# Self-attention stages: which engine copies the turned probabilities out of PSUM

## The chip, the cores and the metric

The kernel runs on one NeuronCore of a Trainium2 chip. The metric is the device time of one execution in microseconds (us). The core has five instruction queues that matter here: TensorE (PE, matrix products and transpositions), VectorE (DVE), ScalarE (ACT), GpSimd (POOL) and SyncE (SP, which issues DMA transfers). Each queue is worked in order, and the queues meet at semaphores.

## The reference

The program is a decoder of four layers over `x` of shape (8, 100, 256): eight sequences of 100 tokens. Each layer has a self-attention (or a substitute for it), a cross-attention and a feed-forward part, twelve stages in all. Three of the stages contain a softmax self-attention with 16 heads of 16 features: `L0_attn`, the inner attention of `L1_ffn` (with relative positions), and a convolved one in `L2_xattn`. What they compute, per sequence and head, is

```python
att = softmax((q @ k.T + positions_or_mask) * scale, axis=-1)   # 100 x 100
out = concat_heads(att @ v) @ wo                                # 100 x 256
x   = layernorm(x + out)
```

The change touches the first two. They are called the first stage (tile names `l0a_`, 19.5 to 108 us of the trace) and the second stage (`l1f_`, 946.8 to 1052 us).

## The kernel before, in words

All three attentions are built by `self_heads` (line 1310). It treats one sequence of the batch per **turn** j, and the 16 heads of a sequence as four **groups** of four heads (G = 4), numbered g = 4j + r. `grouped` (line 1332) is true for the first two stages: there the four heads of a group are exponentiated by one instruction, and GpSimd subtracts the row extremum before it. A group passes through these steps:

1. `scores(j)`, line 1545, TensorE: 32 small products into four PSUM banks, for all four groups of a sequence at once. It waits until the maxima of all groups of the sequence before are done, since these read the banks.
2. `maxima(g)`, line 1777, VectorE: adds mask or positions, writes `s_sb` and the row extremum `nmax`; four pairs of instructions per group. In the second stage the positions come by DMA (`l1f_bd`, line 1421).
3. `shift(g)`, line 1454, GpSimd: subtracts the extremum.
4. `exponentials(g)`, line 1678, ScalarE: one exponential over 100x400 into `probs`. There are three slots of `s_sb` and `probs`.
5. `sums(g)`, line 1793, VectorE: row sums; `inverses(j)`, line 1797, after the fourth.
6. `turn(g)`, line 1569, TensorE: transposes the four heads into PSUM bank 4 or 5, by the parity of g. It waits until the group two before has been copied out of that bank.
7. `copy_turned(g)`: copies the 100x400 result from PSUM to `probsT`. **Even groups are copied by VectorE (line 1786), odd ones by ScalarE (line 1694).** Each counts up a semaphore of its own, `even_copied` or `odd_copied`.
8. `values(j)`, line 1581, TensorE: waits for both counts, and multiplies all four groups with the values.

After that follow, one or two turns behind: `inv` (line 1499, copied by ScalarE on line 1655), `outputs` (line 1802, VectorE), `y` (line 1504, TensorE: output projection), `add_output` (line 1808 with the statistics of lines 114 and 116, VectorE), the reciprocal root on GpSimd (lines 136 and 138), `normalise_vector` (line 123, VectorE), and `turn_x` (line 1509, TensorE, stored by ScalarE on line 1664, in the second stage by two instructions on line 1660). `y`, `inv`, `turn_x`, the values of the next sequence (`v`, line 1489) and a late part of the keys (`k`, line 1484) share one PSUM bank in a fixed order (`wait_side`).

The order on each engine is written out by hand, one `for j in range(B + 2)` loop per engine. In a turn of the grouped stages:

- VectorE: maxima(4j), sums(4j-2), sums(4j-1), inverses(j-1), **copy_turned(4j-2)**, maxima(4j+1), add_output(j-2), maxima(4j+2), normalise(j-2), sums(4j), maxima(4j+3), **copy_turned(4j)**, copy_values(j+1), sums(4j+1), outputs(j-1).
- ScalarE: exponentials(4j), copy_turned(4j-1), exponentials(4j+1), inv(j-1), exponentials(4j+2), a copy of keys in turns 0 and 1, exponentials(4j+3), copy_turned(4j+1), turn_x(j-2).
- TensorE: turn(4j-2), y(j-2), turn(4j-1), values(j-1), inv(j-1), turn(4j), v(j+1), keys in turns 0 and 1, scores(j+1), turn(4j+1), turn_x(j-2).
- GpSimd: shift(4j), widen(j-1) (line 1461), shift(4j+1), the root for j-2, shift(4j+2), shift(4j+3).

Of the kernel before, what the change touches and what calls it, by code (L numbers as in the profile page):

```python
# [14 lines left out]
ACT = mybir.ActivationFunctionType  # L15
AX = mybir.AxisListType

B, S, D = 8, 100, 256
# [1291 lines left out]
def self_heads(nc, st, name, w, bias=None, mask=None, conv=None, xT=None, inner=None, between=None):  # L1310

    H, HD = 16, 16
    G = PER_QUAD
# [5 lines left out]
    with ExitStack() as ctx:  # L1319
        def sb(n, shape, dt=F32):  # L1320
            return ctx.enter_context(nc.sbuf_tensor(f"{name}_{n}", shape, dt))
# [7 lines left out]
        probsT = sb("probsT", [S, 2, G, G * S])  # L1329
        nmax = sb("nmax", [S, 3, G])  # L1330
        rsum, rinv = sb("rsum", [S, B, H]), sb("rinv", [S, B, H])
        grouped = conv is None
# [18 lines left out]
        with stage_sems(nc, sems + stored_sems + NORM_SEMS) as s, nc.Block(no_gpsimd_drain=True) as block:  # L1351
# [3 lines left out]
            turned_tile = lambda g: st.ps[0:S, T_BANK + g % 2, 0:G * S]  # L1355
# [285 lines left out]
            def _(act):  # L1641
# [47 lines left out]
                def copy_turned(g):  # L1689
                    j, r = divmod(g, G)  # L1690
                    act.wait_ge(s.turned, g + 1)
                    if j >= 2:
                        act.wait_ge(s.values_done, j - 1)
                    act.activation(probsT[:, j % 2, r, :], turned_tile(g), ACT.Copy).then_inc(s.odd_copied, 1)

                for part in range(KT):
                    copy_out("k", 0, part)
# [6 lines left out]
                for j in range(B + 2):  # L1704
                    if conv and 1 <= j <= B:
                        exponentials(G * j - 1)
                    if not conv and j < B:
                        exponentials(G * j)
                    if 1 <= j <= B:
                        copy_turned(G * j - 1)  # L1710
                    if j < B:
                        if conv:
                            exponentials(G * j)
                        else:
                            exponentials(G * j + 1)
                    if 1 <= j <= B:
                        copy_out("inv", j - 1)
                    if j == 0 and not between:
                        copy_q(1)
                    if j < B:  # L1720
                        exponentials(G * j + (1 if conv else 2))
                    if j < KT:
                        copy_out("k", 1, j)
                    if j < B:
                        exponentials(G * j + (2 if conv else 3))
                    if j < B:
                        copy_turned(G * j + 1)
                    if j >= 2:
                        copy_out("turn_x", j - 2)

            @block.vector
            def _(dve):
# [48 lines left out]
                def copy_turned(g):  # L1781
                    j, r = divmod(g, G)
                    dve.wait_ge(s.turned, g + 1)
                    if j >= 2:
                        dve.wait_ge(s.values_done, j - 1)
                    dve.tensor_copy(probsT[:, j % 2, r, :], turned_tile(g)).then_inc(s.even_copied, 1)
# [8 lines left out]
                def inverses(j):  # L1795
                    dve.wait_ge(s.summed if grouped else s.exp_done, G * (j + 1))
                    dve.reciprocal(rinv[:, j, :], rsum[:, j, :]).then_inc(s.inv_ready, 1)
# [21 lines left out]
                for j in range(B + 2):  # L1819
                    if j < B:  # L1820
                        if conv:
                            keep(G * j)
                            keep(G * j + 1)
                        else:
                            maxima(G * j)
                    if j == 0 and not between:
                        copy_q(1)
                    if 1 <= j <= B:
                        sums(G * j - 2)
                        sums(G * j - 1)  # L1830
                        inverses(j - 1)
                        copy_turned(G * j - 2)
                    if j < B:
                        maxima(G * j + (0 if conv else 1))
                        if conv:
                            keep(G * j + 2)
                    if j >= 2:
                        add_output(j - 2)
                    if j < B:
                        maxima(G * j + (1 if conv else 2))  # L1840
                    if j < B:
                        if conv:
                            keep(G * j + 3)
                    if j >= 2:
                        if inner:
                            dve.wait_ge(s.x_summed, j - 1)
                        normalise_vector(dve, norm, s, j - 2)
                    sums(G * j)
                    if j < B:
                        maxima(G * j + (2 if conv else 3))  # L1850
                    if conv and 1 <= j <= B:
                        outputs(j - 1)
                    if j < B:
                        copy_turned(G * j)
                    if j + 1 < B:
                        copy_values(j + 1)
                    if conv and j < B:
                        maxima(G * j + 3)
                    sums(G * j + 1)
                    if not conv and 1 <= j <= B:  # L1860
                        outputs(j - 1)
# [2638 lines left out]
```

## Time and profile before

| | |
|---|---|
| median of 3 runs | 2467.63 us (2466.69 to 2467.66) |
| profiled execution | 2466.49 us |
| its span, first to last instruction | 2464.7 us |
| PE busy | 2074.1 us (84%) |
| DVE busy | 1566.5 us (64%) |
| ACT busy | 1062.5 us (43%) |
| POOL busy | 730.9 us (30%) |
| mean granted TensorE clock | 0.902 |

The profiled execution lies 1.14 us below the median, and its span 1.8 us below its own time. The shares of busy time are means over twelve stages with different limits; the two stages of the change take some 190 of the 2465 us. In the views below, a bracket behind a row tells how long the engine stood idle before the instruction and who released it. "PEclk" and granted clock are the TensorE clock as a share of its higher level of 2.4 GHz: 1.00 is that level, 0.50 the lower one of 1.2 GHz.

### The profile page before, as it was taken

To read this page: it belongs to the slowest core of one execution; us is meant where nothing else is said; L and a number is where in the kernel's file an instruction comes from. 1 tells how busy PE (TensorE), PEld (TensorE's weight loads), DVE (VectorE), ACT (ScalarE), POOL (GpSimd) and SP (SyncE) were. 2 spreads that over 40 slices of the span, in tenths; PEclk is the share of its full clock that TensorE was granted. 3 is DMA by queue.
4 is the path that set the end of the run, shared out by engine and by line. 5 is a ranking of instruction groups with operands and counts; after the bars stand their busy time and mean duration, and the time that the engine had idled before them with its cause. 6 is when DMAs were issued, how large, how long until landed. Compare 5 with 4: busy or idle time off the path is not lost. (4 is left out here: it accounts for less than half of the span.)

```text
span 2464.7 us, 41893 instructions
## 1 busy us (share of the span) xinstructions
PE 2074.1 (84%) x14482; PEld 1633.6 (66%) x14482; DVE 1566.5 (64%) x3664; ACT 1062.5 (43%) x2704; POOL 730.9 (30%) x933
## 2 busy tenths in 40 slices
PE   6799578898999984779778969989996899798994
PEld 4567444555666653579756638879995567598893
DVE  5767767895666653755555544556554567557995
ACT  3266456662344442323211635524432367455662
POOL 3543119993000011400122420000002565213546
PEclk9899789999999986889877979979997899798997
DMA  2077126671111125234200024333210367355772
GB/s 117 17 113 109 50 112 171 186 203 66 43 43 46 43 74 167 43 142 153 90 11 5 1 57 115 88 101 97 88 56 29 55 109 102 97 166 180 248 233 82
DMA packets 142725, 240.90 MB, mean 98 GB/s; under 512 B 46999, under 2 KB 108539, under 8 KB 140488
## 3 DMA queue, kind: packets, MB, share of 16 engines
q1 hardware_dynamic: 140492, 235.24, 34.6%
q0 software_dynamic: 2048, 3.29, 0.4%
q8 instruction: 104, 1.70, 0.3%
q14 instruction: 81, 0.66, 0.1%
HBM read 198.35 MB, written 40.12 MB: 97 GB/s over the span
## 5 line engine op out<-in xcount | busy, mean ns | idle before, releaser
L2064 ACT ACTIVATE l1x_probs<-ps,l1x_nmax 100x361 f32<-100x361 f32 x128 | 70.8, 559 | 166.0 <-DVE l1x_nmax L2137 166.0
L2573 POOL TENSOR_TENSOR l1a_dbx<-l1a_dx,l1a_rows 128x400 f32<-128x400 f32 x128 | 130.8, 1049 | 3.0 <-DVE ps L2631 2.2
L2661 PE MATMUL ps<-l1a_zc,tables_sb 128*128 128x400 f32 x256 | 111.1, 519 | 20.4 <-DVE l1a_hs L2618 9.3
L2649 PE MATMUL ps<-ctxT,weights 128*128 128x361 f32 x256 | 101.8, 489 | 10.3 <-PEq L2341 9.3
L3278 PE MATMUL ps<-l3f_routed_x_high,l3f_routed_w_low 128*128 128x128 f32 x320 | 91.5, 286 | 15.4 <-DVE l3f_routed_w_low L3342 14.0
L2855 PE MATMUL ps<-l2f_x_high,l2f_w_high 128*128 128x400 f32 x272 | 95.2, 350 | 0.0
L1145 ACT ACTIVATE l3x_probs<-l3x_s_sb,l3x_nmax 100x361 f32<-100x361 f32 x128 | 75.3, 590 | 44.8 <-DVE l3x_nmax L1250 44.8
L2854 PE MATMUL ps<-l2f_x_high,l2f_w_low 128*128 128x400 f32 x272 | 94.7, 348 | 0.0
L2856 PE MATMUL ps<-l2f_x_low,l2f_w_high 128*128 128x400 f32 x272 | 94.6, 348 | 0.0
L2631 DVE TENSOR_TENSOR_SCAN ps<-ps,l1a_dbx 128x400 f32<-128x400 f32 x86 | 81.8, 986 | 14.5 <-ACT ps L2596 7.3
L3280 PE MATMUL ps<-l3f_routed_x_low,l3f_routed_w_high 128*128 128x128 f32 x320 | 90.8, 284 | 0.0
L3279 PE MATMUL ps<-l3f_routed_x_high,l3f_routed_w_high 128*128 128x128 f32 x320 | 90.8, 284 | 0.0
L1143 ACT ACTIVATE l0x_probs<-ps,l0x_nmax 100x361 f32<-100x361 f32 x128 | 71.0, 562 | 36.8 <-DVE l0x_nmax L1257 36.7
L2661 PEld LDWEIGHTS ps<-l1a_zc,tables_sb 128*128 128x128 f32 x256 | 47.9, 195 | 58.6 <-DVE l1a_zc L2613 17.2
L136 POOL TENSOR_SCALAR l1x_heads_all_vareps<-l1x_heads_all_meanvar 100x1 f32<-100x1 f32 x8 | 1.7, 218 | 279.8 <-DVE l1x_heads_all_meanvar L116 279.8
L2594 ACT ACTIVATE ps<-l1a_delta,weights 128x400 f32<-128x400 f32 x128 | 76.2, 595 | 19.6 <-DVE ps L2631 11.7
L2649 PEld LDWEIGHTS ps<-ctxT,weights 128*128 128x128 f32 x256 | 50.8, 199 | 50.6 <-issue 15.0
L3011 DVE SCALAR_TENSOR_TENSOR l2f_hg<-ps,l2f_biases,l2f_act_out 128x800 f32<-128x800 f32 x34 | 35.7, 1051 | 73.1 <-PE ps L2856 73.1
L3374 POOL TENSOR_TENSOR l3f_routed_w_low<-ctxT,l3f_routed_w_high 128x1024 fp32r<-128x1024 f32 x20 | 49.5, 2475 | 110.2 <-ACT l3f_routed_w_high L3317 110.2
L2137 DVE TENSOR_REDUCE l1x_nmax<-ps 100x2 f32<-100x722 f32 x64 | 58.0, 906 | 34.5 <-PE ps L2000 34.3
L1557 PE MATMUL ps<-l2x_a_kept,l2x_a_taps 100*100 100x100 f32 x768 | 76.0, 258 | 3.0 <-DMA l2x_a_taps<-l2x_taps_spread 2.6
L1557 PEld LDWEIGHTS ps<-l2x_a_kept,l2x_a_taps 100*100 100x100 f32 x768 | 74.3, 174 | 5.5 <-DMA l2x_a_taps<-l2x_taps_spread 3.3
(735 smaller groups left out, 6650.2 us busy)
## 6 DMA issues: line engine op xcount, KB each, us to landing
l1a_rows<-l1a_rows_spilled SPq DMA_DIRECT2D x64, 400.0 KB, 4.4
ctxT<-l_ffn_units SPq DMA_DIRECT2D x20, 1026.0 KB, 5.8
l3f_expert<-l_ffn_units SPq DMA_DIRECT2D x20, 1026.0 KB, 5.9
l2x_a_taps<-l2x_taps_spread SPq DMA_DIRECT2D x8, 1912.5 KB
l2f_landing<-l_ffn_units SPq DMA_DIRECT2D x17, 771.0 KB, 5.4
l1f_gates<-l1f_gates SPq DMA_DIRECT2D x16, 800.0 KB, 4.1
l1x_keys<-l1a_key_sb SPq DMA_DIRECT2D x64, 180.5 KB, 4.6
l1x_kT<-l1x_keys SPq DMA_DIRECT2D x64, 180.5 KB, 2.3
```

The lines of the kernel that those rows point to most:

```text
L1557: last = pe.matmul(score_bank(r)[:, n, :], taps[:, j % 2, first:first + S], kept[:, g % 3, n, c:c + S], start=(c == 0), stop=(c == 2))
L2573: pool.tensor_tensor(dbx[:, n % BUFS, :], dx[:, m, :], rows[:, g % RING, 0, :], ALU.mult).then_inc(s.dbx_ready, 1)
L2594: act.activation(da(n), delta_h[:, m, j, :], ACT.Exp, scale=a_log[:, m, i:i + 1]).then_inc(s.da_ready, 1)
L2631: dve.tensor_tensor_scan(z(n), da(n), dbx[:, n % BUFS, :], 0.0, ALU.mult, ALU.add).then_inc(s.scan_done, 1)
L2649: last = pe.matmul(key_bank(u), w_key[:, k, pair * P:(pair + 1) * P], st.ctxT[:, b, k, :], start=(k == 0), stop=(k == KT - 1))
L2661: pe.matmul(y_bank(m), st.ident, zc[:, n % DONE, :], start=(i == 0), stop=(i == NS - 1)).then_inc(s.sum_done, 1)
L2854: pe.matmul(out, r(w_lo), r(x_hi), start=start, stop=False)
L2855: pe.matmul(out, r(w_hi), r(x_hi), start=False, stop=False)
L2856: return pe.matmul(out, r(w_hi), r(x_lo), start=False, stop=stop)
L3278: pe.matmul(out, r(lo), r(x_high[i % 2][:, k, :]), start=(k == 0), stop=False)
L3279: pe.matmul(out, r(hi), r(x_high[i % 2][:, k, :]), start=False, stop=False)
L3280: last = pe.matmul(out, r(hi), r(x_low[i % 2][:, k, :]), start=False, stop=(k == KT - 1))
```

## The change

In the grouped stages ScalarE makes all 32 copies of turned probabilities of a stage, where it made the 16 of the odd groups; the 16 of the even groups leave VectorE. ScalarE's `copy_turned` now counts up the semaphore of the group's parity. copy_turned(4j-2) stands at the head of ScalarE's turn, before exponentials(4j); copy_turned(4j) stands between exponentials(4j+2) and exponentials(4j+3), behind the copy of the keys in turns 0 and 1. The convolved stage keeps its order.

```diff
@@ block.scalar
-                    act.activation(probsT[:, j % 2, r, :], turned_tile(g), ACT.Copy).then_inc(s.odd_copied, 1)
+                    act.activation(probsT[:, j % 2, r, :], turned_tile(g), ACT.Copy).then_inc((s.even_copied, s.odd_copied)[g % 2], 1)
...
                     if conv and 1 <= j <= B:
                         exponentials(G * j - 1)
+                    if grouped and 1 <= j <= B:
+                        copy_turned(G * j - 2)
                     if not conv and j < B:
                         exponentials(G * j)
...
                     if j < KT:
                         copy_out("k", 1, j)
+                    if grouped and j < B:
+                        copy_turned(G * j)
                     if j < B:
                         exponentials(G * j + (2 if conv else 3))
@@ block.vector
                         inverses(j - 1)
-                        copy_turned(G * j - 2)
+                        if not grouped:
+                            copy_turned(G * j - 2)
...
-                    if j < B:
+                    if not grouped and j < B:
                         copy_turned(G * j)
```

## Rows read from the trace of the kernel before

**Rows 1.** Window, its length, busy PE, PEld, DVE, ACT, POOL, then PEclk: first stage

```profile
40.71:84.88 44.17, 31.86 (x474) 24.14 (x474) 42.39 (x225) 17.72 (x40) 22.89 (x35) 1.00 0.01 2
```

**Rows 2.** Grouped lines of the first stage: busy us, mean ns, idle before

```profile
L1777 DVE CUSTOM_DVE_ANT_0 l0a_s_sb<-ps,tables_sb 100x100 f32<-100x100 f32 x128 | 25.4, 255 | 6.6 <-PE ps L1545 6.6
L1786 DVE COPY l0a_probsT<-ps 100x400 f32<-100x400 f32 x16 | 8.6, 540 | 1.2 <-PE ps L1569 1.2
L1694 ACT ACTIVATE l0a_probsT<-ps 100x400 f32<-100x400 f32 x16 | 8.0, 501 | 4.2 <-PE ps L1569 3.7
```

**Rows 3.** Timeline of DVE, first stage, one turn: start us, us

```profile
49.57 0.25 DVE L1777 CUSTOM_DVE_ANT_0 l0a_s_sb<-ps,tables_sb 100x100 f32<-100x100 f32 x1
...
51.54 0.51 DVE L1786 COPY l0a_probsT<-ps 100x400 f32<-100x400 f32 x1
51.97 0.25 DVE L1777 CUSTOM_DVE_ANT_0 l0a_s_sb<-ps,tables_sb 100x100 f32<-100x100 f32 x1
...
56.12 0.25 DVE L1777 CUSTOM_DVE_ANT_0 l0a_s_sb<-ps,tables_sb 100x100 f32<-100x100 f32 x1
...
56.84 0.56 DVE L1786 COPY l0a_probsT<-ps 100x400 f32<-100x400 f32 x1
57.33 0.41 DVE L1751 COPY l0a_vals<-ps 100x256 f32<-100x256 f32 x1
...
58.40 0.25 DVE L1777 CUSTOM_DVE_ANT_0 l0a_s_sb<-ps,tables_sb 100x100 f32<-100x100 f32 x1
```

**Rows 4.** Timeline of PE, first stage: values, scores and output around that turn's end

```profile
54.55 1.11 PE L1489 MATMUL ps<-weights,XT 128*100 128x256 f32 x4 [0.19 <-ACT l0a_r_sb L1655]
57.07 0.96 PE L1545 MATMUL ps<-l0a_kT,l0a_q_pad 32*100 32x100 f32 x32 [1.41 <-DVE l0a_nmax L1777]
...
59.33 1.11 PE L1504 MATMUL ps<-weights,l0a_o_norm 128*100 128x256 f32 x4 [0.31 <-ACT XT L1664]
```

**Rows 5.** Timelines of PE and DVE, first stage: maxima that waited for scores

```profile
39.68 0.96 PE L1545 MATMUL ps<-l0a_kT,l0a_q_pad 32*100 32x100 f32 x32
...
40.71 0.26 DVE L1777 CUSTOM_DVE_ANT_0 l0a_s_sb<-ps,tables_sb 100x100 f32<-100x100 f32 x1 [1.88 <-PE ps L1545]
```

**Rows 6.** Timelines of ACT and POOL, first stage, the end of that turn

```profile
58.95 0.33 ACT L1664 ACTIVATE XT<-ps 128x200 f32<-128x200 f32 x1
...
59.29 0.85 POOL L1454 TENSOR_TENSOR l0a_s_sb<-l0a_s_sb,l0a_nmax 100x400 f32<-100x400 f32 x1 [1.43 <-DVE l0a_nmax L1777]
...
60.17 0.54 ACT L1678 ACTIVATE l0a_probs<-l0a_s_sb 100x400 f32<-100x400 f32 x1 [0.90 <-POOL l0a_s_sb L1454]
```

**Rows 7.** Timelines of ACT and PE, first stage, turn 1

```profile
33.75 0.48 ACT L1694 ACTIVATE l0a_probsT<-ps 100x400 f32<-100x400 f32 x1
...
34.33 0.89 PE L1581 MATMUL ps<-l0a_probsT,l0a_vals 100*32 100x100 f32 x32 [1.20 <-DVE l0a_probsT L1786]
```

**Rows 8.** Timeline of PE, end of the first stage

```profile
94.40 2.03 PE L1504 MATMUL ps<-weights,l0a_o_norm 128*100 128x256 f32 x4 [0.67 <-ACT XT L1664]
```

**Rows 9.** Busy time by window, second stage: turns 3 to 6 together, turn 5

```profile
988.34:1027.10 38.76, 28.49 (x379) 21.44 (x377) 34.26 (x182) 16.42 (x37) 21.03 (x32) 0.91 0.32 67
1007.78:1017.29 9.51, 6.37 (x96) 4.79 (x94) 8.47 (x46) 4.15 (x10) 5.26 (x8) 0.99 0.32 68
```

**Rows 10.** Timeline of DVE, second stage

```profile
978.82 0.26 DVE L1777 CUSTOM_DVE_ANT_0 l1f_s_sb<-ps,l1f_bd 100x100 f32<-100x100 f32 x1 [15.05 <-DMA l1f_bd<-l1f_positions]
...
986.05 0.25 DVE L1777 CUSTOM_DVE_ANT_0 l1f_s_sb<-ps,l1f_bd 100x100 f32<-100x100 f32 x1
...
1020.69 0.42 DVE L1808 TENSOR_TENSOR l1f_heads_all_resid<-ps,X 100x256 f32<-100x256 f32 x1 [0.20 <-PE ps L1504]
```

**Rows 11.** Timeline of PE, second stage: values, scores, output

```profile
984.75 1.86 PE L1489 MATMUL ps<-weights,l1f_xT 128*100 128x256 f32 x4
...
996.50 1.65 PE L1545 MATMUL ps<-l1f_kT,l1f_q_pad 32*100 32x100 f32 x32 [1.77 <-DVE l1f_nmax L1777]
...
1018.66 1.99 PE L1504 MATMUL ps<-weights,l1f_o_norm 128*100 128x256 f32 x4 [0.25 <-ACT l1f_xT L1660]
```

## The prediction

> **What bounds the kernel now.** I read the stages one by one, because the change touches two of twelve. First the busy time by window, with one window per turn, then grouped lines, then the timelines of single engines over one turn, since the question is which wait ends last there.
>
> In the first stage, turns 2 to 6 take 44.17 us together, 8.83 us each, and VectorE is busy for 42.39 of them; ScalarE only for 17.72 [rows 1]. In the timeline VectorE's instructions follow one another with hardly a gap, so **VectorE sets the turn**. The copies to be moved are 16 of 0.54 us on VectorE; the like copy on ScalarE takes 0.50 [rows 2]. TensorE waits for VectorE: before the scores of the next sequence it stands idle for 1.41 us, until the last maxima of this one are done [rows 4].
>
> The second stage is different at its start: the first maxima of turn 2 wait 15.05 us for the positions' transfer and begin at 978.82 us [rows 10]. What is saved ahead of that is lost. From turn 3 on it is the first stage again: four turns take 38.76 us, a clean one 9.51, with VectorE busy for 8.47 of it [rows 9].
>
> **The change, part by part.** *What leaves VectorE.* In its queue an instruction costs the distance between starts, not its duration. copy_turned(4j-2) starts at 51.54 and the maxima behind it at 51.97: 0.43 us. copy_turned(4j) starts at 56.84 and its successor at 57.33: 0.49 us [rows 3]. If nothing else ended later, a turn would take 8.83 - 0.92 = 7.91 us.
>
> *What is late next.* The scores of the next sequence can only start when the maxima of 4j+3 are done, and the next maxima need the scores. From rows: those maxima begin at 56.12 [rows 3], the scores at 57.07 and take 0.96 [rows 4], so 0.95 + 0.96. Where maxima did wait, they began 0.07 us after the scores' end (39.68 + 0.96 = 40.64, then 40.71) [rows 5]. That makes 1.98 us from one group of maxima to the next sequence's first. VectorE now takes 58.40 - 56.12 = 2.28 us for this piece [rows 3]; without the copy it takes 1.79. So 0.19 us of the second copy comes back as a wait for scores: a turn of **8.10 us, 0.73 less**. Bounds of this term: 0 if the scores start sooner, 0.19 as taken.
>
> *Is TensorE ready to start the scores earlier?* The product before them, the next values, starts at 54.55 and ends at 55.66 [rows 4]; the scores would start 0.43 us sooner, at 56.64. Relative to the previous scores that chain doesn't move, and the turn may shorten by 1.41 us before it touches. The output projection ends at 59.33 + 1.11 = 60.44, 4.32 us after the maxima's 56.12 [rows 3, 4]; the new VectorE order wants it 1.98 us and then 2.68 us after those maxima (51.97 - 49.57 = 2.40, less the copy's 0.43, and 0.72 for one more group of maxima as between 56.12 and 56.84 [rows 3]), that is at 4.66. No wait.
>
> *What ScalarE gains.* Two copies of 0.50 us per turn [rows 2] on an engine that is busy for 3.5 of 8.8 us [rows 1]. What matters is who stands behind them. copy_turned(4j-2) stands before exponentials(4j): ScalarE is free for it when the XT store ends, 58.95 + 0.33, and done with it some 0.4 us later, at about 59.7. The input of the exponentials, the shift on GpSimd, ended at 60.14 and the exponentials began at 60.17 [rows 6]; in the new order the shift ends 0.30 us sooner, at 59.84. The copy fits with about 0.1 us to spare. In the second stage the store is two activations (line 1660); with 0.33 us for the second, as here, the exponentials would start up to 0.3 us late; who waits for them is the row sum five VectorE steps later and a transposition more than 2 us later, so I take 0 and keep 0.3 us a turn as the upper bound. copy_turned(4j) stands before exponentials(4j+3), whose input comes 1.74 us after the group's maxima began (58.40, 60.14 [rows 3, 6]); its transposition is over before those maxima start, so it is done in time. values(j) is released by the odd copy on ScalarE at 33.75 + 0.48 = 34.23, followed by the product at 34.33 [rows 7], although the profile names VectorE's copy there: the even copies are not what ends last, and none of their 0.54 us can be won at that place. No DMA and nothing on SP or GpSimd is moved; the convolved stage keeps its code.
>
> *Sum of the first stage.* Turn 0 is a chain of TensorE and key copies: 0. Turn 1: between 0 and 0.43 us, since the values' product is fixed by ScalarE [rows 7] and only what follows moves; I take 0.2. Turns 2 to 6: 44.17 - 5 x 8.10 = 3.7 us. Turn 7 has no next scores, and its second copy lies behind the last maxima; what ends last there is the exponentials, the XT store and the output projection at 94.40 [rows 8], so only the first copy counts: 0.4. Sum **4.3 us**.
>
> *Sum of the second stage.* Turns 0 and 1: 0, as the transfer sets 978.82 [rows 10]. Turn 2: the scores would start 0.95 - 0.10 us behind maxima at 986.05 - 0.43, that is at 986.47, but the values' product ends at 984.75 + 1.86 = 986.61 [rows 10, 11]; so scores at 986.65, their end at 987.61, maxima at 987.68 instead of 988.34 [rows 9]: 0.7. Turns 3 to 6: a clean turn of 9.51 loses the same 0.73, and 0.05 comes back, the price of a semaphore, because the output projection, behind a store 0.33 us longer, ends at 4.32 + 0.33 = 4.65 us where VectorE wants it at 4.66: 8.83. In these four turns the trace also shows dips of the granted clock: scores of 1.65 us instead of 0.96 after an idle 1.77 us, and an output projection of 1.99 us instead of 1.11, for which VectorE waits 0.20 [rows 4, 10, 11]. They make up most of the distance between 38.76 and 4 x 9.51 = 38.04. In the new turn the idle time before scores is 0.7 us shorter, as short as or shorter than the 1.41 us behind which the clock of the first stage stays at 1.00 [rows 1, 4]. So I take them as gone: 38.76 - 4 x 8.83 = 3.4. If both stay, two turns gain 0.7, one 0.4 and one nothing: 1.8. Turn 7: 0.4. Sum **4.5 us**, bounds 2.9 and 4.5.
>
> Together 8.8 us. The profiled execution took 2466.49 us and would take 2457.7; the median shown stands 1.14 us higher, and 2467.6 - 8.8 = **2458.8 us**. A measurement of this kernel can tell about 0.2%, 4.9 us, from no change, so this is faster by 0.36%.
>
> **The rivals.**
>
> *TensorE takes the turn over.* With two copies less VectorE is no longer far ahead, and where the granted clock falls to 0.50 the path over scores and output projection ends last. Its price: 0.69 us for cold scores and 0.88 for a cold output [rows 4, 11]. A first-stage turn would be 8.10 + 0.69 = 8.79, no gain; with the dips in all turns of the first stage and the known ones in the second the sum is 0.2 + 0.2 + 0.4 + 0.7 + 1.8 + 0.4 = 3.7 us: 2463.9 us, inside what can't be told from no change. For it: the second stage has such dips. Against: the first had 1.00 through five turns, and shorter turns leave TensorE less idle. Chance 0.18, of which about half ends within 0.2%.
>
> *ScalarE's queue becomes the path: slower.* Each copy stands in front of exponentials. If TensorE's transposition ended after the shift of those exponentials, every copy would be added to the chain maxima, shift, exponentials, sums: 32 x 0.50 us = 16 us added, of which VectorE's 8.8 us are to be taken off: about 2475 us. It decides from the point where a copy delays the exponentials by more than the 2 us after which their result is first wanted. Rows 6 show about 0.1 us of room and no delay; the second stage may see 0.3. Chance 0.04. The Trainium skill speaks for this side: "TensorEngine Tiling (Array Packing)", section "PSUM Bottleneck", advises to use ScalarE and VectorE together for emptying PSUM. By that rule the move would cost. The trace doesn't bear it out here: ScalarE has 5.3 of 8.8 us free in a turn, VectorE 0.4 [rows 1].
>
> *More than forecast.* If the scores begin sooner than 0.95 us behind the maxima's start, the 0.19 us of ten turns stays won: 8.8 + 1.9 = 10.7 us, 2456.9 us. Against it: this distance is the duration of four maxima and a semaphore, and both stay. Chance 0.08.
>
> **How the numbers follow.** The forecast has 0.70. Range: below, the 2456.9 of the last rival and the 1 us by which single runs differ; above, the 2463.9 of the first. I give 2456.0 to 2464.0, which leaves out the slower rival and the edges. Faster by over 0.2%: nearly all of 0.70, 0.08 and half of 0.18, 0.85. Within 0.2%: 0.11. Slower: 0.04.
>
> **What would show it.** Right: no copy of `probsT` on VectorE in either stage and 32 on ScalarE; turns of about 8.1 us in the first stage and 8.8 in the second; a new wait of 0.1 to 0.2 us before the first maxima of a turn, released by the scores of line 1545; the wait for the positions' transfer longer, with its end at the same distance from the stage's start; the exponentials of the first stage still released by GpSimd. Wrong: exponentials released by ScalarE's own queue with sums waiting behind them; VectorE waiting for the output projection by more than 0.1 us in most turns; scores of 1.65 us in the first stage; or turns shortened as said and the time given back in a later stage.

## The result, and the profile after

The changed kernel takes **2453.31 us** (median of 20 executions, 2449.28 to 2464.06) where the kernel before, run beside it, took 2466.98 us (20, 2461.14 to 2479.2). The ratio is 0.9949 [0.9937, 0.9961]. It is faster, as forecast, and the time lies below the forecast range of 2456.0 to 2464.0.

The difference of the two medians, 13.7 us, overstates what the change is worth. Over all executions made for this document the kernel before has a mean of 2465.2 us (114 executions, standard error 0.4) and the changed kernel one of 2455.3 us (36, standard error 0.8): **9.9 us less**, with an error of 0.9. That pools series in which only the kernel before was timed with others. In the three series that timed both side by side the means differ by 11.3, 11.2 and 12.8 us, each with an error of 1.6 to 1.9. So the gain is known as 9 to 12 us, and no closer. The executions of one kernel scatter by 3 to 5 us (standard deviation), and the profiled one of the changed kernel happened to take 2463.35 us. So what follows compares parts of the program, and traces of several executions.

The profiled execution after, by engine:

```profile
span 2461.5 us, 41893 instructions
PE 2079.2 (84%) x14482; PEld 1638.0 (67%) x14482; DVE 1556.0 (63%) x3632; ACT 1074.6 (44%) x2736; POOL 730.4 (30%) x933
```

The 32 copies are where they should be: 32 instructions fewer on VectorE, 32 more on ScalarE, 10.5 us less busy time on the one, 12.1 more on the other. The sum of all 41893 instructions is the same. Grouped lines of the first stage:

```profile
L1694 ACT ACTIVATE l0a_probsT<-ps 100x400 f32<-100x400 f32 x32 | 15.9, 500 | 6.0 <-PE ps L1569 5.7
L1678 ACT ACTIVATE l0a_probs<-l0a_s_sb 100x400 f32<-100x400 f32 x32 | 17.2, 538 | 22.2 <-POOL l0a_s_sb L1454 22.2
```

The exponentials' wait is still put down to GpSimd's shift alone, 22.2 of 22.2 us: the copies in front of them don't hold them up. By window, as in [rows 1, 9] (turns 2 to 6 of the first stage; turns 3 to 6 of the second; turn 5 of the second; the columns are those of [rows 1]):

```profile
42.90:83.04 40.14, 31.46 (x470) 23.75 (x470) 38.37 (x215) 22.21 (x50) 22.93 (x35) 1.00 0.01 2
988.05:1023.75 35.70, 25.99 (x378) 19.67 (x379) 30.82 (x172) 18.78 (x44) 21.04 (x32) 0.99 0.34 70
1006.13:1014.94 8.81, 6.37 (x96) 4.79 (x96) 7.70 (x44) 4.83 (x12) 5.26 (x8) 1.00 0.36 72
```

The first stage's five turns took 44.17 us and take 40.14; the second's four took 38.76 and take 35.70, a clean one 8.81 where it was 9.51. The granted clock is 1.00 in the first stage as before; over the second's four turns it is 0.99 where it was 0.91.

How a turn of the first stage now ends on VectorE, and the scores it waits for (timelines of VectorE, then of TensorE):

```profile
57.01 0.25 DVE L1781 CUSTOM_DVE_ANT_0 l0a_s_sb<-ps,tables_sb 100x100 f32<-100x100 f32 x1
...
57.73 0.41 DVE L1755 COPY l0a_vals<-ps 100x256 f32<-100x256 f32 x1
58.07 0.55 DVE L1797 TENSOR_REDUCE l0a_rsum<-l0a_probs 100x4 f32<-100x400 f32 x1
58.54 0.35 DVE L1806 TENSOR_TENSOR l0a_o_norm<-ps,l0a_r_sb 128x200 f32<-128x200 f32 x1
58.97 0.26 DVE L1781 CUSTOM_DVE_ANT_0 l0a_s_sb<-ps,tables_sb 100x100 f32<-100x100 f32 x1
```

```profile
57.95 0.96 PE L1545 MATMUL ps<-l0a_kT,l0a_q_pad 32*100 32x100 f32 x32 [0.67 <-DVE l0a_nmax L1781]
```

The values' copy follows the maxima directly. From one group of maxima (57.01) to the next turn's first (58.97) are 1.96 us; the scores end at 57.95 + 0.96 = 58.91, and the maxima begin 0.06 us later. The last step, from 58.54 to 58.97, is 0.43 us long for an instruction whose successor elsewhere starts 0.27 us behind it (the experiment with the head copy alone, below): here lies the new wait, 0.16 us. The idle time ahead of the scores fell from 1.41 to 0.67 us.

This turn, the one that the prediction had read, is the exception. In the other four of turns 2 to 6 the same step is 0.35 us and the wait **0.08 us**, in all five traces of the changed kernel; the mean is 0.10. The kernel before shows why: there the scores begin 0.95 us behind the start of the last maxima in turn 3 [rows 3, 4], but 0.85 to 0.86 us behind it in turns 2, 4, 5 and 6. Turn 4 of the kernel before (timelines of VectorE, then of TensorE):

```profile
64.94 0.25 DVE L1777 CUSTOM_DVE_ANT_0 l0a_s_sb<-ps,tables_sb 100x100 f32<-100x100 f32 x1
65.80 0.96 PE L1545 MATMUL ps<-l0a_kT,l0a_q_pad 32*100 32x100 f32 x32 [1.31 <-DVE l0a_nmax L1777]
```

ScalarE at the head of a turn, first stage and then second stage (timelines of ScalarE):

```profile
51.98 0.51 ACT L1694 ACTIVATE l0a_probsT<-ps 100x400 f32<-100x400 f32 x1
52.69 0.54 ACT L1678 ACTIVATE l0a_probs<-l0a_s_sb 100x400 f32<-100x400 f32 x1 [0.20 <-POOL l0a_s_sb L1454]
...
1006.98 0.76 ACT L1660 ACTIVATE l1f_xT<-ps,weights 128x100 f32<-128x100 f32 x2
1007.62 0.51 ACT L1694 ACTIVATE l1f_probsT<-ps 100x400 f32<-100x400 f32 x1
1008.00 0.56 ACT L1678 ACTIVATE l1f_probs<-l1f_s_sb 100x400 f32<-100x400 f32 x1
```

```profile
1007.03 0.85 POOL L1454 TENSOR_TENSOR l1f_s_sb<-l1f_s_sb,l1f_nmax 100x400 f32<-100x400 f32 x1 [1.05 <-DVE l1f_nmax L1781]
```

In the first stage the copy leaves 0.20 us to spare. In the second, where the store is two activations, GpSimd's shift ends at 1007.88 and the exponentials start at 1008.00, right behind the copy: they are some 0.1 us late, and the turn is 8.81 us all the same.

In the second stage another wait is the longer one. The output projection, which stands behind the longer store, ends at 1007.79 + 1.11 = 1008.90, and VectorE adds it to the residual at 1008.94 (timelines of TensorE, then of VectorE):

```profile
1007.79 1.11 PE L1504 MATMUL ps<-weights,l1f_o_norm 128*100 128x256 f32 x4 [0.73 <-ACT l1f_xT L1660]
1008.61 0.26 DVE L1781 CUSTOM_DVE_ANT_0 l1f_s_sb<-ps,l1f_bd 100x100 f32<-100x100 f32 x1
1008.94 0.42 DVE L1812 TENSOR_TENSOR l1f_heads_all_resid<-ps,X 100x256 f32<-100x256 f32 x1
```

That step is 0.33 us long where it is 0.18 in the kernel before, a wait of **0.15 us**. It stands in turns 4 to 6 of all five traces of the changed kernel, and not with only one copy of a turn moved. The wait for the scores is 0.08 us in the clean turns here too. Another wait, 0.94 us for GpSimd's addition ahead of line 123, stands in these turns before and after alike.

**Where the time went, over several traces.** Six traces of the kernel before (the one shown ahead of the prediction and five of the next section) and five of the changed kernel give these mean times, stage parts bounded by the first maxima of a turn. The rows add up to 19 us less than the span in either kernel, since no row holds the second stage's tail:

| part | before | after | difference |
|---|---|---|---|
| first stage, turns 0 and 1 | 21.74 | 22.20 | +0.46 |
| first stage, turns 2 to 6 | 44.20 | 40.13 | -4.07 |
| first stage, turn 7 to its last maxima | 6.53 | 6.09 | -0.44 |
| first stage, tail | 16.74 | 16.53 | -0.2 |
| second stage, start to turn 0 | 57.76 | 57.82 | +0.06 |
| second stage, turns 0 and 1 | 32.36 | 31.91 | -0.45 |
| second stage, turn 2 | 9.67 | 9.60 | -0.07 |
| second stage, turns 3 to 6 | 39.31 | 35.60 | -3.7 |
| second stage, turn 7 to its last maxima | 7.40 | 6.92 | -0.48 |
| rest of the program | 2210.28 | 2210.30 | 0.0 |
| mean span | 2464.95 | 2456.1 | -8.9 |

The rest of the program runs from 2207.0 to 2212.7 us in the six traces of before and from 2207.5 to 2214.1 in the five of after. That is scatter, nearly as large as the gain, and the difference of 0.0 has an error of 1.9 us. In the first profile of after it (2214.07) and the two first turns (23.82) hide most of the gain. The two turns at each stage's start scatter as well (20.97 to 23.82 us; 31.27 to 33.55). Two small rows hang on single traces: the first stage's tail is 16.7 us in four of the five traces of after, as before, and 15.7 in one; and turn 7 of the second stage takes 7.2 to 7.3 us in five of the six of before and 8.11 in one, so that its usual gain is 0.3 us.

### The profile page after: what moved, and what is told of

Same layout as the page of the kernel before. It is cut to its first block and busy times, and to the rows that moved or that the text cites. A ratio compares the mean times of both kernels' runs of the same rounds, so it can differ in the third digit from the quotient of the medians.

```text
span 2461.5 us, 41893 instructions
## 1 busy us (share of the span) xinstructions
PE 2079.2 (84%) x14482; PEld 1638.0 (67%) x14482; DVE 1556.0 (63%) x3632; ACT 1074.6 (44%) x2736; POOL 730.4 (30%) x933
## 3 DMA queue, kind: packets, MB, share of 16 engines
HBM read 198.35 MB, written 40.12 MB: 97 GB/s over the span
```

## The experiments

Theory A: VectorE's time is the gain, less the wait for scores; 4 to 5 us in either stage. Theory B: the gain is something else than the copies' time on VectorE (the granted clock, or a shift of the rest of the program). Runs of an unedited kernel measure the scatter. All ratios are to the kernel before, run beside.

### Both kernels again

The changed kernel and the kernel before, each once more, unedited.

> The changed kernel once more, unaltered, for a second trace and times beside the kernel before. The turns' lengths are fixed by instruction durations: about 8.0 us in turns 2 to 6 of the first stage and 8.8 in turns 4 to 6 of the second, as in the first trace. Theory A (the gain beyond 8.8 us is a matter of where TensorE's low-clock stretches fall, and differs from execution to execution): turns 0 and 1 of the first stage take either about 12.0 and 9.0 us (clock 1.00) or 12.6 and 11.2 (clock 0.50), and the ratio over five rounds lies anywhere from 0.994 to 0.998. Theory B (a gain of some 4 us more that is always there): ratio 0.9949 again, and a stretch outside the two stages that is shorter by some us than before in every trace.

> A control: the kernel before, unaltered, timed against itself. If single executions only scatter, its ratio is 1.000 within its interval, and turns are 8.83 and 9.5 to 9.9. If the ratio is 0.998 or less, the comparisons of this series favour whatever is set against the kernel before by that much, and the surplus of the single moves (7 to 10 us measured against 4 to 5 worked out) is none of the change's.

The changed kernel: 0.9955 [0.9938, 0.9972], 2454.62 us against 2464.61. The kernel before against itself: 1.0004 [0.9986, 1.0022]. The first stage repeats to 0.02 us (40.12 us after, 44.15 before). The second stage of the kernel before doesn't: windows over turns 3 to 6, and over turn 6 alone, of this second trace of it:

```profile
993.74:1035.53 41.79, 32.94 (x377) 24.79 (x378) 34.47 (x180) 16.00 (x36) 21.00 (x32) 0.79 0.28 61
1023.37:1035.53 12.16, 11.28 (x95) 8.50 (x96) 8.89 (x45) 3.81 (x9) 5.25 (x8) 0.50 0.21 49
```

One turn ran wholly at the lower clock, 0.50, and took 12.16 us instead of 9.51. TensorE, VectorE in that turn (timelines):

```profile
1025.41 2.03 PE L1504 MATMUL ps<-weights,l1f_o_norm 128*100 128x256 f32 x4 [0.24 <-ACT l1f_xT L1660]
1033.79 1.67 PE L1545 MATMUL ps<-l1f_kT,l1f_q_pad 32*100 32x100 f32 x32
```

```profile
1027.47 0.42 DVE L1808 TENSOR_TENSOR l1f_heads_all_resid<-ps,X 100x256 f32<-100x256 f32 x1 [0.90 <-PE ps L1504]
1033.90 0.42 DVE L1751 COPY l1f_vals<-ps 100x256 f32<-100x256 f32 x1 [1.03 <-PE ps L1489]
1035.53 0.26 DVE L1777 CUSTOM_DVE_ANT_0 l1f_s_sb<-ps,l1f_bd 100x100 f32<-100x100 f32 x1 [0.46 <-PE ps L1545]
```

At the lower clock TensorE sets the turn, and VectorE waits for it three times. So the dips of the clock, which I had priced at 0.7 us from one profile, cost more in some executions. That had to be settled by more traces.

### The scatter of the second stage: more traces of either kernel

Single profiled executions, four of the kernel before and two of the changed one, and one more timing of the changed one.

> One more trace of the kernel before. Theory A: turns 3 to 6 of the second stage hold a stretch at 0.50 and one turn of more than 10 us in most executions (about 40.5 us for four turns; 38.8 in the first trace was the short end). Outside the two stages: 2210.8 and 2212.7 us so far; if the rest of the program is part of the surplus, it stays above 2210.

> One more trace of the changed kernel. Theory A: four turns of the second stage in 35.7 us, no stretch at 0.50 in them, five turns of the first in 40.1. Outside the two stages 2208 and 2214 us so far; an always shorter rest would put it below 2208.

> As r10_none_look: four turns of the second stage in more than 40 us rather than 38.8, with a stretch at 0.50; the rest of the program above 2210 us if it is part of the surplus, scattered like the changed kernel's if not.

> The changed kernel again, with a third series of times. If the gain is 9 to 10 us (turns 4.5 us in the first stage, 4 to 5 in the second), the ratio is 0.9960 to 0.9963; if the surplus is always there, 0.995. Rest of the program: below 2209 us if it is part of the gain, anywhere from 2207 to 2214 if it scatters.

> The kernel before. Turns 3 to 6 of the second stage anywhere from 38.0 to 41.8 us (never below 38.0, four clean turns). Rest of the program 2210 to 2213 us as in four traces, or lower, if it scatters like the changed kernel's.

> The changed kernel. Turns 3 to 6 of the second stage 35.3 to 35.8 us with no stretch at 0.50 in turns 4 to 6. Rest of the program as for r13_both.

> The kernel before once more: turns 3 to 6 of the second stage 38.0 to 41.8 us; rest of the program 2210 to 2213 us if that is a property of this kernel, anywhere from 2203 to 2214 if it scatters.

Turns 3 to 6 of the second stage, one window of each trace: the kernel before in its best and in a poor execution, then the changed kernel in one:

```profile
992.10:1030.14 38.04, 25.89 (x378) 19.49 (x378) 34.02 (x180) 16.58 (x36) 21.02 (x32) 0.99 0.31 68
```

```profile
988.84:1029.38 40.54, 30.85 (x377) 23.25 (x378) 34.28 (x180) 16.26 (x36) 21.01 (x32) 0.84 0.30 63
```

```profile
986.18:1021.84 35.66, 26.08 (x378) 19.75 (x378) 30.82 (x172) 18.73 (x44) 20.98 (x32) 0.98 0.33 70
```

The six traces of before have 38.76, 41.79, 38.05, 38.40, 38.28 and 40.55 us, the five of after 35.41 to 35.70. VectorE's busy time hardly differs within either kernel, TensorE's does: 25.89 us at 0.99, 30.85 at 0.84. So the dips cost the kernel before nothing to 3.7 us in these turns, 39.31 - 38.04 = 1.3 on average. The best execution had its dip too, only later: the clock fell at 1029.2 us, 1 us before turn 6 ended, and turn 7 ran at 0.50 up to its last maxima, 8.11 us instead of 7.22:

```profile
1030.14:1038.25 8.11, 7.22 (x57) 5.68 (x57) 6.26 (x34) 2.68 (x8) 4.40 (x7) 0.50 0.01 3
```

Counted over the traces of the next sections too: where the second stage had lost copies on VectorE, none of nine traces has the clock at 0.50 between the start of turn 4 and the last maxima of turn 7. Where VectorE's load there was unchanged or given back, all eight traces without added work on TensorE have it there, and the one with such work (below) doesn't.

The measured ratio of the changed kernel in this series was 0.9952 [0.9932, 0.9971] (2454.15 us), and the single executions came out at 2455.94 and 2460.68 us for it and 2469.07, 2468.23, 2462.8 and 2464.16 us for the kernel before.

### One stage alone

```diff
+        moved = grouped and name == "l0a"
...
-                    if grouped and 1 <= j <= B:
+                    if moved and 1 <= j <= B:
                         copy_turned(G * j - 2)
```

The other kernel has "l1f" there. `moved` takes the place of `grouped` in the four conditions of the change.

> Copies moved in the first stage alone; the second keeps VectorE's even copies. My steps: 4.3 us less than before (ratio 0.9983), turns 2 to 6 of the first stage at 8.0, those of the second at 9.5 to 9.9 as before. Theory B would show more here, 6 us or more, if the surplus hangs on the first stage's earlier end. Theory A: the turns as said, and the total within some us of 4.3, according to the clock.

> Copies moved in the second stage alone. My steps: 3 to 4.5 us less (ratio 0.9982 to 0.9988); turns 3 to 6 of the second stage at 8.8, of the first at 8.83. The wait of the maxima of turn 2 for the positions' transfer ends at the same distance from the stage's start. If the two single moves sum to less than the whole move, the surplus comes from their meeting; if they sum to it, it is in one of them.

First stage alone: 0.9971 [0.996, 0.9983]; second stage alone: 0.9959 [0.9943, 0.9975]. Added, the two ratios give 17 us, more than the 9.9 of both; either interval is 5 us wide and more, so the ratios can't split the gain. The windows can (first stage, second stage; the kernel with the first stage moved, then the one with the second):

```profile
40.80:80.92 40.12, 31.47 (x470) 23.75 (x470) 38.36 (x216) 22.16 (x50) 22.88 (x35) 1.00 0.01 2
985.12:1025.93 40.81, 30.99 (x377) 23.41 (x378) 34.23 (x181) 16.23 (x36) 20.99 (x32) 0.83 0.29 63
```

```profile
42.69:86.86 44.17, 31.87 (x474) 24.16 (x474) 42.41 (x225) 17.70 (x40) 22.84 (x35) 1.00 0.01 2
989.87:1025.56 35.69, 25.85 (x378) 19.53 (x379) 30.82 (x173) 18.76 (x44) 21.01 (x32) 0.99 0.34 71
```

Each stage is that of the changed kernel where it was changed (40.12, 35.69) and that of the kernel before where it wasn't (44.17; 40.81 with a turn at 0.50). The stages are independent of each other. Each ratio is larger than what its stage shows, 7.1 and 10.1 us against 4.6 and 4.3 (the section on what the stages don't hold, below).

### One copy of a turn alone

```diff
+        head_moved, mid_moved = grouped and True, grouped and False
...
-                    if grouped and 1 <= j <= B:
+                    if head_moved and 1 <= j <= B:
                         copy_turned(G * j - 2)
...
-                    if grouped and j < B:
+                    if mid_moved and j < B:
                         copy_turned(G * j)
```

VectorE's two conditions follow. The other kernel has the two values exchanged.

> In both stages only copy_turned(4j-2) is moved, to the head of ScalarE's turn; copy_turned(4j) stays on VectorE. My steps: 0.43 us less per turn in full, since no wait for scores arises (2.28 us of VectorE work against a scores path of 1.98): first-stage turns 8.83 - 0.43 = 8.40, second-stage clean turns 9.08; in all 14 turns, about 5 to 5.5 us less. Rival (ScalarE's exponentials are delayed by the copy ahead of them and something waits): turns over 8.5 and 9.2.

> Only copy_turned(4j) is moved; copy_turned(4j-2) stays on VectorE. My steps: 0.49 us of VectorE's time goes, 0.19 comes back as a wait for scores: first-stage turns 8.83 - 0.30 = 8.53, second-stage clean turns 9.2, and nothing in turn 7; about 3.5 us less in all, and the waits before the first maxima of a turn released by the scores. If the scores' wait were no limit, the turns would be 8.34 and 9.0.

Head copy alone: 0.996 [0.9944, 0.9975]; middle copy alone: 0.9969 [0.995, 0.9987]. Windows of the head copy's kernel, then of the middle copy's:

```profile
40.86:82.89 42.03, 31.87 (x474) 24.15 (x474) 40.19 (x221) 20.24 (x45) 22.85 (x35) 1.00 0.01 2
989.21:1025.91 36.70, 26.37 (x382) 20.06 (x383) 32.27 (x177) 17.93 (x40) 20.99 (x32) 0.99 0.32 69
```

```profile
40.26:82.56 42.30, 31.46 (x470) 23.76 (x470) 40.45 (x221) 20.09 (x45) 22.84 (x35) 1.00 0.01 2
985.61:1022.16 36.55, 25.62 (x378) 19.29 (x379) 32.45 (x177) 17.72 (x40) 20.98 (x32) 1.00 0.32 70
```

Against the mean of 44.20 us the first stage's turns 2 to 6 lose 2.17 us by the head copy (0.43 each, the distance of starts in [rows 3]) and 1.90 by the middle one (0.38 each, of 0.49). Together 4.07, just what both give. The 0.11 that is missing sits where it was forecast, behind the middle copy, and is about the mean wait of 0.10. The end of a turn on VectorE, head copy's kernel and middle copy's kernel:

```profile
57.36 0.35 DVE L1807 TENSOR_TENSOR l0a_o_norm<-ps,l0a_r_sb 128x200 f32<-128x200 f32 x1
57.63 0.25 DVE L1782 CUSTOM_DVE_ANT_0 l0a_s_sb<-ps,tables_sb 100x100 f32<-100x100 f32 x1
```

```profile
56.82 0.35 DVE L1807 TENSOR_TENSOR l0a_o_norm<-ps,l0a_r_sb 128x200 f32<-128x200 f32 x1
57.25 0.26 DVE L1782 CUSTOM_DVE_ANT_0 l0a_s_sb<-ps,tables_sb 100x100 f32<-100x100 f32 x1
```

0.27 us without the wait, 0.43 with it (0.35 in the other turns): the scores come late only when the middle copy is gone, for it alone lies between maxima(4j+3) and the next turn. In the second stage's clean turns the head copy gives 0.47 us (9.04) and the middle one 0.39 (9.12), but both together only 0.70, because the wait for the output projection arises only then.

### VectorE's time given back

ScalarE makes all copies, as in the change; VectorE executes, where its copies stood, a reduction over a table whose result nothing uses.

```diff
+                def spend(i):
+                    dve.tensor_reduce(spent[:, i:i + 1], st.tables[0:S, 0:342], AX.X, ALU.add)
...
+                        else:
+                            spend(2 * j - 1)
...
+                    if grouped and j < B:
+                        spend(2 * j)
```

> All copies on ScalarE as in the changed kernel, but VectorE spends the freed time: where each copy stood it sums 342 columns of a constant table into a tile that nobody reads (about 0.43 us from start to start; 32 such instructions in all, which compute nothing that is used). If all of the gain comes through VectorE's queue, the turns are back at 8.8 and 9.5 and the ratio at 0.9995 to 1.0005, or what the control shows. If part of it comes from the copies being made earlier or faster on ScalarE, the turns are shorter than that; if the copies on ScalarE cost something, longer.

0.9986 [0.9969, 1.0003], 2461.18 us. Windows of both stages, and the added instruction among the grouped lines of the first:

```profile
44.69:88.22 43.53, 31.80 (x473) 24.09 (x473) 41.77 (x225) 21.71 (x49) 22.84 (x35) 1.00 0.01 2
989.31:1029.91 40.60, 31.79 (x382) 24.20 (x382) 33.98 (x181) 19.09 (x44) 20.98 (x32) 0.82 0.30 63
```

```profile
L1794 DVE TENSOR_REDUCE l0a_spent<-tables_sb 100x1 f32<-100x342 f32 x16 | 7.6, 475 | 0.0
```

The turns of the first stage are back at 8.71 us, 0.12 below the old 8.83, as the two reductions take 0.37 and 0.42 us from start to start where the copies took 0.43 and 0.49; the second stage is back at 40.60 with a turn at 0.50. With all 32 copies on ScalarE and VectorE nearly as loaded as before, the turns are back: their gain is VectorE's time, and **ScalarE's added copies cost the turns nothing**. The Trainium skill, "TensorEngine Tiling (Array Packing)", section "PSUM Bottleneck", advises sharing the emptying of PSUM between ScalarE and VectorE. For these copies the case doesn't bear it out: splitting them costs 9 to 12 us, since VectorE is the engine that sets the turn. VectorE goes on reading scores, values and outputs from PSUM, so emptying PSUM by one engine alone was not tried.

### Work for TensorE instead of a shorter turn

The kernel before, with two more products in each of turns 0 to 6 of the second stage, ahead of the next scores; their result is used by nothing. If the dips come from TensorE's idle time there, they should go.

```diff
+                    if name == "l1f" and j + 1 < B:
+                        for _ in range(2):
+                            pe.matmul(st.ps[0:S, T_BANK + 1, 0:342], st.ident[0:S, 0:S], st.tables[0:S, 0:342], start=True, stop=True)
```

> The kernel before, with two matrix products over constants (342 columns, results unused) on TensorE in the second stage, between the next values and the scores, where it otherwise stands idle for 1 to 1.8 us behind VectorE. Nothing is taken from VectorE. Theory A (the second stage's long turns are TensorE's clock falling because it stands idle): no stretch at 0.50 in turns 3 to 6, four turns of 9.5 us, 38.0 in all against 40.6 to 41.8 in three of the four traces with unshortened turns, and about 2.5 us less in the whole kernel (ratio 0.999). Rival (the long turns have another cause, the shortened turns avoid it by themselves): a turn of 12.16 us is still there, or the products only add time.

1.0012 [0.9999, 1.0024]: no gain. Windows over turn 2 and over turns 3 to 6, and TensorE in turn 2 and in turn 4:

```profile
980.98:992.40 11.42, 8.61 (x82) 6.07 (x83) 8.56 (x46) 2.88 (x6) 5.25 (x8) 0.55 0.24 56
992.40:1030.44 38.04, 30.51 (x398) 22.25 (x398) 34.02 (x181) 16.58 (x36) 21.02 (x32) 1.00 0.28 59
```

```profile
988.71 2.49 PE L1633 MATMUL ps<-tables_sb 100*100 100x342 f32 x4
...
1008.25 1.32 PE L1633 MATMUL ps<-tables_sb 100*100 100x342 f32 x4
```

The clock was 1.00 in turns 3 to 6, the four turns took 38.04 us, and turn 7 ran without a dip (7.21 us to its last maxima). None of the eight traces with VectorE's load and without the filler is without a dip up to there, so this speaks for TensorE's idle time as the cause; one trace doesn't show it. Turn 2, which begins behind the long wait for the positions at the lower clock, paid for it: the filler takes 2.49 us there and stands in front of the scores, 11.42 us instead of the mean of 9.67. My expectation, which counted the dips and not turn 2, missed. So what makes the clock fall stays open, with one trace for the idle time.

### Further in the same direction

The changed kernel, with copy_values on ScalarE too and sums(4j) moved behind maxima(4j+3), so that VectorE has less and the scores are released sooner. On ScalarE copy_values(j+1) stands ahead of the keys' copy of turns 0 and 1 and of copy_turned(4j). The diff shows ScalarE's order first, then VectorE's.

```diff
+                    if grouped and j + 1 < B:
+                        copy_values(j + 1)
...
-                    sums(G * j)
...
+                    sums(G * j)
...
-                    if j + 1 < B:
+                    if not grouped and j + 1 < B:
                         copy_values(j + 1)
```

> Changed kernel, and further: the row sums of group 4j stand behind the maxima of 4j+3 instead of ahead of them, and the copy of the next values is made by ScalarE. If the scores path (1.98 us) is what sets the end of a turn now, as the waits say, 0.48 us of sums behind the maxima fill the wait, and VectorE's piece behind those maxima is 0.48 + 0.47 + 0.27 + about 0.7 = 1.9 us: turns of about 7.5 us in the first stage and 8.3 in the second, 13 turns by 0.5 us, some 6 us below the changed kernel. If VectorE's total were the limit, moving the sums alone would do nothing and the turns would fall by 0.33 us only.

**0.9924 [0.9899, 0.9949], 2445.39 us: faster than both kernels.** The windows:

```profile
39.41:77.24 37.83, 31.54 (x470) 23.83 (x470) 36.06 (x211) 24.07 (x55) 22.86 (x35) 1.00 0.01 2
977.57:1011.34 33.77, 25.85 (x378) 19.53 (x379) 29.18 (x169) 19.92 (x48) 21.00 (x32) 0.99 0.35 71
```

The first stage's turn is 7.57 us, with VectorE busy for 7.21 of it and ScalarE for 4.81: another 0.46 us a turn, and the second stage's four turns lose 1.8 us more. The turns are close to what was expected, 7.5 and 8.3 us (8.44 measured in the second stage). The time is 10.5 us below the changed kernel's mean (six executions) where I had expected some 6.

### What the stages don't hold

Every kernel with copies moved came out faster than its stages show: the ratios of the single moves give 7.1, 10.1, 9.9 and 7.6 us (first stage, second stage, head copy, middle copy), the stages 4 to 6 us. With VectorE's time given back the median is 3.4 us lower though the turns are back, while the unedited kernel against itself gives 1.0004. Each of these has an error of about 2 us, and several share one series of the kernel before, so this may be scatter. It may as well be some 2 to 3 us won in the rest of the program by every kernel with such an edit. The traces don't decide it: the rest of the program is on average no shorter in the five traces of the changed kernel (error 1.9 us), and 3.8 us shorter (error 1.8) in the six of the other kernels with copies moved. This part of theory B stays open.

## Why the prediction was right and where it failed

**VectorE sets the turn, and a copy costs the distance of starts: right.** 0.43 us for the head copy, measured alone. Giving the time back took the turns' gain away.

**The scores come late: right; by 0.19 us: twice too much.** The wait is 0.08 us in four turns of five and 0.16 in the fifth, 0.10 on average. The term rests on the 0.95 us between the last maxima's start and the scores, read in turn 3, the one turn of five where it is 0.95; in the other four of the same trace it is 0.85 or 0.86, and the sum for turn 2 of the second stage took 0.95 - 0.10. So half of what the rival "more than forecast" describes came true, against the argument that this distance stays. Turns of 8.03 us instead of the 8.10 forecast; turns 2 to 6 gave 4.07 us instead of 3.7.

**ScalarE has room: right.** 0.20 us ahead of the exponentials in the first stage where 0.1 was forecast; in the second they start some 0.1 us late, within the bound of 0.3. The slower rival is out. "TensorE takes the turn over" came true in turn 2 of the second stage (below) and, at the full clock, by a little: VectorE waits 0.15 us for the output projection in each of turns 4 to 6, one of the signs named for "wrong".

**First stage, the rest.** Turn 7 gave 0.44 (forecast 0.4), and the tail is as before in four of five traces. Turn 1 gave 0.1 (forecast 0.2): 9.18 us before, 9.07 to 9.09 in four traces of after, and 11.18 in the fifth. Turn 0 takes 12.0 to 13.1 us before and 11.9 to 13.8 after. A mean of 4.6 us in the parts that are steady, forecast 4.3.

**Second stage, turns 0 and 1: 0 stands within the scatter.** I had said that the wait for the positions' transfer would grow, and it didn't: it was 15.05 us [rows 10] and is 13.99 (timeline of VectorE).

```profile
978.45 0.26 DVE L1781 CUSTOM_DVE_ANT_0 l1f_s_sb<-ps,l1f_bd 100x100 f32<-100x100 f32 x1 [13.99 <-DMA l1f_bd<-l1f_positions]
```

Over all traces it is 14.2 to 15.7 us before and 14.0 to 14.7 after; why it didn't grow stays open.

**Second stage, turn 2: this step failed.** I had 0.7 us, and it is 0.07. TensorE of the changed kernel there, and VectorE's first maxima behind it:

```profile
984.39 2.00 PE L1489 MATMUL ps<-weights,l1f_xT 128*100 128x256 f32 x4
986.32 1.67 PE L1545 MATMUL ps<-l1f_kT,l1f_q_pad 32*100 32x100 f32 x32
```

```profile
988.05 0.26 DVE L1781 CUSTOM_DVE_ANT_0 l1f_s_sb<-ps,l1f_bd 100x100 f32<-100x100 f32 x1 [0.46 <-PE ps L1545]
```

The scores do follow the values' product directly, as I wrote. But they started while the clock was still at the lower level that I had seen in that product, and took 1.67 us, not the 0.96 that I had put there. (In the trace of before the clock had just risen, at 986.3 us, and the scores that began at 986.90 took 0.96.) TensorE ends last, and at 0.50 it takes back what VectorE had won. The turn takes 9.60 us in all five traces, against 9.52 in the trace from which I forecast.

**Second stage, turns 3 to 6: 3.4 forecast, 3.7 measured, for partly other reasons.** A clean turn lost 0.70 us (9.51 to 8.81, forecast 8.83), 2.8 in all. That it fits is luck: the wait for the output projection is 0.15 us where I had 0.05, called "the price of a semaphore", which no run shows, and the wait for the scores is 0.08 where I had 0.19. Both go back to the same 0.95: the projection ends 4.66 us behind the last maxima's start (1004.24 to 1008.90), as I had worked out, but VectorE, less held up by the scores, is ready for it at 4.55. The first of the four is 0.3 to 0.4 us longer than a clean one in four of the five traces (9.25 us in the one shown; it begins before the clock has risen again). And the dips, which I took as worth 0.7 us from one profile and as gone, were gone, but were worth 1.3 on average and up to 3.7. That they went was right nine times of nine; the reason I gave, TensorE's shorter idle time before the scores, is not shown, though the one trace with the filler speaks for it. Turn 7 gave 0.48, forecast 0.4, of which 0.15 is the dip in one trace of before.

**The sum was 8.8 us; the traces' spans give 8.9, the times 9.9 pooled and 11 to 13 side by side.** By stage it was 4.6 us where I had 4.3, and 4.3 where I had 4.5: turn 2's missing 0.6 was in part made up by dips that cost more than I had read.

**What put the time outside the range was how the range was built.** The step that failed is its lower edge, "the 2456.9 of the last rival and the 1 us by which single runs differ". Three executions that agree within 1 us said little about a kernel whose single executions scatter by 3 to 5. I took the absolute time from their median, 2467.6; the kernel's mean over 114 executions is 2465.2, 2.4 us lower. The pooled gain was 1.1 us larger than the sum, and the 20 executions of the result have a median 2.0 us below the changed kernel's mean: 2458.8 - 2.4 - 1.1 - 2.0 = 2453.3. None of the three did it alone. With the anchor's 2.4 us back the time would be 2455.7, still outside; the kernel before, run beside the changed one, had a median of 2467.0, close to my anchor; and the changed kernel's mean, 2455.3, lies under 2456.0 too. A surplus of 1 to 3 us over the stages' 8.9 may be part of it and stays open (above).

## What to carry to other kernels

Cost an instruction that leaves a saturated queue by the distance between starts, then look for the next producer that its consumer waits for; here that pair of rows gave the turn to 0.1 us. Read such a distance in several turns of the trace: the one read here was the odd one of five, and doubled the term. Decide by busy share of the stage which engine makes the copies, not by sharing evenly. And when a forecast is an absolute time, its range must hold the scatter of single executions, which a median of three doesn't show; a stretch where the clock falls has to be read in several traces before it gets a price.

## What the runs showed of the hardware

The granted clock in a stretch of the same kernel differs between executions. Turns 3 to 6 of the unchanged second stage took 38.05 to 41.79 us in six traces. In turns 4 to 7 TensorE's clock went to 0.50 in each of them, for some 3.4 us or so long that a whole turn ran at it (12.16 us instead of 9.51); what differs is when it fell and for how long. With turns of 8.4 to 9.1 us, VectorE having lost copies, nine traces show no such stretch from turn 4 to the last maxima. Outside the two stages the rest of the program varied between 2207.0 and 2214.1 us over eleven traces, a large part of why single executions differ.

A copy of 100x400 f32 out of PSUM takes 0.50 us on ScalarE and 0.54 on VectorE [rows 2], and VectorE's next instruction starts 0.43 to 0.49 us behind its start [rows 3].
